# A fused log-attention block: GpSimd clips one half of a step's exponentials, VectorE the other

## The reference, cut to what matters

```
L   = einsum('bhqd,bhkd->bhqk', q, k) * scale
L_y = einsum('bhqd,bhkd->bhqk', q, k_y) * scale
agg = sum(exp(clip(L_y, -15, 15)) * mask, axis=-1) + EPS
r   = log(abs(L) + EPS) - log(agg + EPS)
w   = softplus(r) * mask
A   = w / (sum(w, axis=-1) + EPS)
out = einsum('bhqk,bhkd->bhqd', A, v)
```

## Time and profile before

| | us |
|---|---|
| median of 3 runs (range) | 1131.52 (1123.58 to 1134.69) |
| the profiled execution | 1128.8 |
| its span | 1127.1 |
| PE busy | 898.9 (80% of the span) |
| DVE busy | 675.2 (60%) |
| ACT busy | 594.7 (53%) |
| POOL busy | 540.5 (48%) |

### The profile page before, as it was taken

The page is one execution under the profiler, slowest core; times in us unless marked ns, Lnnn a source line. Parts: engine busy times, 40 slices in busy tenths (PEclk is TensorE's granted clock), DMA queues, the critical chain, the costliest instruction groups (busy, mean ns, idle before and its releaser), DMA issues.

```text
span 1127.1 us, 19899 instructions
## 1 busy us (share of the span) xinstructions
PE 898.9 (80%) x6851; PEld 535.3 (47%) x6851; DVE 675.2 (60%) x1444; ACT 594.7 (53%) x853; POOL 540.5 (48%) x758
## 2 busy tenths in 40 slices
PE   4777665899986778888888888888788776999991
PEld 2566554766664323333333334333344335766661
DVE  4778854522132466988888887788745864422334
ACT  1232124145544577978787878888653233245551
POOL 1112068682083455655543332343311577877784
PEclk9888978899989688999999999999856587999996
DMA  9950001224224577574646363632210002122434
GB/s 294 259 79 1 1 27 40 73 71 119 76 76 148 152 210 210 144 213 112 193 124 181 101 186 106 191 112 64 76 38 1 19 31 78 41 78 79 145 96 146
DMA packets 114111, 123.74 MB, mean 110 GB/s; under 512 B 13296, under 2 KB 76272, under 8 KB 113888
## 3 DMA queue, kind: packets, MB, share of 16 engines
q1 hardware_dynamic: 96224, 100.54, 32.2%
q0 software_dynamic: 8416, 17.29, 4.8%
q10 hardware_dynamic: 9376, 4.65, 1.4%
HBM read 59.71 MB, written 62.72 MB: 109 GB/s over the span
## 4 chain that ended last, share of the span: by engine, by line
PE 56%; DVE 21%; issue 10%; ACT 5%; DMA 4%; POOL 2%; SPq 2%; DVEq 0%; POOLq 0%; ACTq 0%
PE psum L807 10%; PE psum L1753 8%; PE psum L1705 6%; DVE ring_b L1971 6%; PE psum L830 5%; PE psum L1737 5%; PE psum L778 3%; PE psum L767 3%; PE psum L820 3%; PE psum L1771 2%; DVE parts L1978 2%; PE psum L1786 2%; PE psum L735 1%; PE psum L789 1%; ACT r_rows L901 1%
## 5 line engine op out<-in xcount | busy, mean ns | idle before, releaser
L1971 DVE TENSOR_SCALAR ring_b<-psum 128x1024 int32<-128x1024 int32 x160 | 195.5, 1222 | 75.4 <-PE psum L1705 75.2
L1845 ACT ACTIVATE ring_a<-psum 128x1024 f32<-128x1024 f32 x160 | 163.1, 1024 | 90.5 <-PE psum L1705 89.7
L2080 POOL TENSOR_SCALAR_AFFINE_SELECT ring_b<-ring_b 128x512 f32<-128x512 f32 (+1 forms) x112 | 84.4, 768 | 232.3 <-ACT ring_b L1851 232.0
L1851 ACT ACTIVATE ring_b<-ring_b 128x1024 f32<-128x1024 f32 x160 | 168.4, 1053 | 48.3 <-DVE ring_b L1971 48.3
L1705 PE MATMUL psum<-stacks 32*128 32x128 f32 (+3 forms) x1024 | 105.5, 392 | 58.3 <-DVE ring_b L1971 37.1
L1438 DVE TENSOR_TENSOR ring_b<-psum,ring_b 128x512 f32<-128x512 f32 x72 | 49.2, 684 | 159.2 <-ACT ring_b L933 156.8
L807 PE MATMUL psum<-w_expert,ring_a 128*128 x284 | 134.9, 597 | 2.5 <-ACT ring_a L948 1.5
L1705 PEld LDWEIGHTS psum<-stacks 32*128 32x128 f32 x1024 | 60.4, 195 | 154.6 <-issue 61.1
L1963 DVE TENSOR_SCALAR ring_a<-ring_a 128x1024 f32<-128x1024 f32 x160 | 119.3, 749 | 22.9 <-ACT ring_a L1845 22.7
L2080 POOL TENSOR_SCALAR_AFFINE_SELECT ring_a<-ring_a 128x512 f32<-128x512 f32 (+1 forms) x112 | 81.5, 741 | 43.5 <-DVE ring_a L1963 43.5
L1753 PE MATMUL psum<-ring_b,values 128*32 128x256 f32 (+3 forms) x1024 | 94.4, 480 | 4.0 <-DVE oT L2016 4.0
(11 more groups left out here) (210 smaller groups left out, 1417.5 us busy)
## 6 DMA issues: line engine op xcount, KB each, us to landing
stack_q<-parts SPq DMA_DIRECT2D x32, 256.0 KB
stack_ky<-parts SPq DMA_DIRECT2D x32, 256.0 KB
stacks<-stack_q SPq DMA_DIRECT2D x64, 128.0 KB
stacks<-stack_ky SPq DMA_DIRECT2D x64, 128.0 KB
stack_k<-parts SPq DMA_DIRECT2D x32, 256.0 KB
stacks<-stack_k SPq DMA_DIRECT2D x64, 128.0 KB
stack_qr<-parts SPq DMA_DIRECT2D x32, 256.0 KB
stacks<-stack_qr SPq DMA_DIRECT2D x64, 128.0 KB
```

Source lines behind the costliest of these rows:

```text
L1845: nc.scalar.activation(exps[:, n % RING, 2 * u:2 * u + 2, :], psum[:, first:first + 2, :], ACT.Exp, scale=SCALE).then_inc(self.exp, 1)
L1851: nc.scalar.activation(part, part, ACT.Ln, bias=1.0).then_inc(self.ln, 1)
L1971: nc.vector.tensor_scalar(ring[:, m % RING, HEADS_B[u][0]:HEADS_B[u][1] + 1, :].bitcast(I32), psum[:, first:first + 2, :].bitcast(I32), 0x ...
L2080: ins = nc.gpsimd.affine_select(out=part, in_=part, pattern=[[0, part.ap[1][1]], [1, 128]], compare_op=ALU.is_ge, fill=0.0, base=0, channe ...
```

## The change

`clip_exps` keeps only half 0 and stays after `abs_scores(m, 1)`. Half 1 is clipped by GpSimd in `pool_step`, between the mask of B's step and the mask of A's step, with the same two-operation `tensor_scalar`. It waits for both exponentials of the step. It counts on `mask_a` too, and A's mask waits for that count (its own engine's clip) and for DVE's clip of half 0; so `mask_a` has two counts for a step, and `sum_exps` waits for 2n + 2.

```diff
@@ sum_exps
-                pe.wait_ge(self.mask_a, n + 1)
+                pe.wait_ge(self.mask_a, 2 * n + 2)
@@ clip_exps
-            def clip_exps(self, v, n, u):
-                v.wait_ge(self.exp, 2 * n + u + 1)
-                part = exps[:, n % RING, 2 * u:2 * u + 2, :]
+            def clip_exps(self, v, n):
+                v.wait_ge(self.exp, 2 * n + 1)
+                part = exps[:, n % RING, 0:2, :]
                 nc.vector.tensor_scalar(part, part, CLIP_LO, CLIP_HI, ALU.max, ALU.min).then_inc(self.clip, 1)
@@ vector_step
-                if 0 <= n - 1 < STEPS_A:
-                    self.clip_exps(v, n - 1, 1)
@@
-                    self.clip_exps(v, n, 0)
+                    self.clip_exps(v, n)
@@ pool_step
                 if 0 <= n - 1 < STEPS_A:
-                    p.wait_ge(self.clip, 2 * n)
+                    p.wait_ge(self.exp, 2 * n)
+                    part = exps[:, (n - 1) % RING, 2:4, :]
+                    nc.gpsimd.tensor_scalar(part, part, CLIP_LO, CLIP_HI, ALU.max, ALU.min).then_inc(self.mask_a, 1)
+                    p.wait_ge(self.mask_a, 2 * n - 1)
+                    p.wait_ge(self.clip, n)
                     self.mask(p, exps[:, (n - 1) % RING], (n - 1) % DUS).then_inc(self.mask_a, 1)
```

## The result

| | before | after |
|---|---|---|
| median, us (runs) | 1132.88 (4) | 1268.36 (4) |
| lowest to highest | 1123.58 to 1134.69 | 1263.6 to 1269.75 |
| ratio (95% interval) | | 1.121 (1.117 to 1.126) |

The changed kernel is 12% slower, 137 us by the ratio. The forecast was 1146.5 us, the range ended at 1178.

What follows compares the result with a forecast made beforehand. No engine alone was the bound: PE was nearest, and the rest was lost in hand-overs. Port collisions of 12 us in six batches plus 3 us for A's mask made 15 us on 1131.5, so 1146.5 us; range 1129 to 1178 us.

Steps and rivals of the forecast that it cites:

- No engine alone is the bound, hand-overs are; half 1's clip is not in one: Batch of ten steps, 58.3 us: PE nearest the bound; removing half 1's clip from DVE saves at most 0.88 us.
- The clip's own time, 1.09 us: Each of 80 added 128x1024 clips on POOL takes 1.09 us, like POOL's mask of the same size.
- rival B: POOL's clip is dear, 2.75 us: A's mask overruns its room in nearly every step, 40 to 81 us; chance 0.10.
- The own-engine wait, 0.08 us: A's mask, behind POOL's clip, waits for a semaphore of its own engine: 0.08 us.
- The room of A's mask, and what hides the overrun: 3 us: A's mask ends 1.17 us later; PE's sums pay in full about 4 times, counted as 3 us of 4.7.
- Steps 0 to 15, set against the 0.88 us that goes: First steps, mask directly behind a 0.4 us longer clip: their cost about equals the 0.88 us saved, less its own collisions.
- The port, 2.0 us a batch: POOL's instructions and DVE's SBUF operations take turns, delaying five places in a batch: 2.0 us, 12 us for six.
- The clock would go down behind longer gaps: PE's clock might drop behind the longer gap at 518.23: up to 1.7 us more a batch, 8 to 10 in all.
- Rival A: The added work is covered; only places where the mask is last pay, 2 to 5 us, 1131 to 1137 us; chance 0.30.
- Rival C: DVE's relief wins: half 1's absolute values start earlier and B's masks collide less, up to 5 us faster, 1126; chance 0.07.

Runs made afterwards that it cites:

- 256 columns: The changed kernel with GpSimd clipping only 256 of half 1's 1024 columns, the others unclipped: 1139.87 us, 1.006 of the kernel before.
- the select: The changed kernel with a select that keeps every element in place of GpSimd's clip, half 1 unclipped: 1139.15 us, 1.007 of the kernel before.
- max alone: The changed kernel with only max in GpSimd's clip, so half 1 isn't bounded above: 1222 us, 1.078 of the kernel before.
- 512 columns: The changed kernel with GpSimd clipping 512 of half 1's 1024 columns, the others unclipped: 1172.6 us, 1.035 of the kernel before.

## Why the prediction was wrong, point by point

- *No engine alone is the bound, hand-overs are; half 1's clip is not in one.* Right. Without that clip the time is the same (0.998, 0.995 to 1.002), and the moved clip of half 0 shortened just the gaps that the chain named.
- *The clip's own time, 1.09 us.* **This step failed**, and it makes nearly all of the error. "The clip has one input, as the mask and the cast have, so I take 1.09 us"; the runs showed 3.62 us, alone as in the kernel. It was bounded by the nearest rows: a select and a cast from below, a two-input operation from above (2.75 us). None of those rows has the clip's operations, max and min, and these set the price; where the instruction takes 1.06 us (256 columns), the loss is 7 us instead of 137. The upper bound wasn't one: the clip is dearer, and a two-input add of this size itself takes 2.34 us. "A two-operation instruction of this engine is in no row" stood there, as the point for rival B, with one chance in ten. The estimate after the Trainium skill, "GPSIMD Engine Reference", section 3.1 (ports bound a body of two operations, 0.88 us and a dispatch) fits multiply and add, 1.05 us, and is wrong for max and min.
- *The own-engine wait, 0.08 us.* Right (604.38 to 604.46).
- *The room of A's mask, and what hides the overrun: 3 us.* Too small, in a sum that came out too large. With the select, 16 products of the sums waited for A's mask between 500 and 790 us, 14.0 us, where the prediction counted four places in all; but PE then waited 7.6 us less for absolute values, which it didn't count. That the whole is 7 to 8 us is in part luck.
- *Steps 0 to 15, set against the 0.88 us that goes.* Right for a short clip (61.4 us instead of 59.5), and a term that failed with the price: 36 us at 3.62 us.
- *The port, 2.0 us a batch.* Right in kind for an instruction that collides as the mask does: `divide` and the split stretched, half 0's clips took 0.9 us, as drawn. Too large in size: the select cost 8 us in all, not 15, the gap at `project_out` grew by 0.2 us, not 0.4, and the batches by 2.9, 1.7, 0.2, 2.3 and 0.4 us. For the actual clip the term is mostly wrong in kind too, since half 0's clips run beside it: 46 of the 80 lay wholly inside GpSimd's clip, with a mean of 0.71 us, and 27 overlapped a mask, with a mean of 1.02 us. Over all 80 it is 0.82 us.
- *Rival B: "between half and all of it is paid".* Its mechanism is at work, from 1.9 us on as written (1.035 there). With the measured 3.62 us its rule gives an overrun of 3.62 + 0.08 - 1.57 = 2.13 us, times 64 steps 68 to 136 us. That the upper end is nearly the 137 us measured is luck: those 64 steps lost 94 us, about 0.7 of the whole, inside the rule's range, and 36 us came from the first 16 steps, which the rule leaves out. With max alone the 64 steps lost 69 us (rule: 41 to 82), with 512 columns 34 (13 to 27). The rule also has no engine that is full. In the batch from 566 us POOL is, and PE takes 6 us more at a granted clock of 0.88 instead of 0.97. How the excess of the steps without a fetch splits between the chain and the clock was not tried.
- *The clock would go down behind longer gaps.* Named as a risk, at the price assumed. With the select it didn't come: from step 16 to 78 PE was busy 303 us against 302 before. In the changed kernel PE was busy 334 us there, at a granted clock of 0.87 up to step 39 and 0.91 behind it, against 0.96 and 0.98.
- *Rival A* is about what happens at the price assumed. There the select's 8 us lie between its 2 to 5 and the forecast's 15, but by its own sign, half 0's clips at 0.75 us or less, it isn't the case: they took 0.9. *Rival C* is out.

## What to carry to other kernels

Price a moved instruction by its operation, not by its shape: if no row of the trace has that operation on that engine, the price is open upwards, and one run of that instruction alone would have shown it here. Take work off an engine only where that work stands in a hand-over: 55 us of VectorE's time gave nothing that could be measured. Sum up what an engine does in each stage apart: GpSimd had room in the stretch that the prediction read, and none in the first 16 steps with a 3.62 us clip. If a sum comes out near the measured time, look whether the time arose where the sum put it. And an engine that waits 232 us is not free if others wait behind the added work: count the room from its end to who needs it.

## What the runs showed of the hardware that was not expected

- GpSimd's `tensor_scalar` on 128x1024 fp32 takes 3.62 us with max and min, 2.77 with max alone, 1.05 with multiply and add.
- A GpSimd instruction doesn't always exclude VectorE's in-place clip for its whole length. Back to back with selects, a VectorE clip took 1.41 us instead of 0.69 and a select 1.37 instead of 1.04; beside the slow clip VectorE lost 0.7 us in five clips of 12, though each GpSimd clip lasted over 4 us. The Trainium skill, "SBUF — State Buffer", section "Who interferes with whom", lets the second one block fully until the first has ended. The selects fit that, the clips don't, and the measurement decides.
- Where VectorE's clips follow each other without a pause, both sides pay: a GpSimd clip took 4.2 to 4.4 us beside them and 3.62 alone. A single one costs little: in the changed kernel, of the 46 GpSimd clips with a whole VectorE clip inside them, the median took 3.62 us.
